# Key maxima of the last tile over all 128 rows with zero-padded keys, bias rows moved from ScalarE's queue to SyncE's, and new order tables

## The chip, the cores and the metric

The kernel runs on one core of a Trainium2 chip. The metric is the device time of one execution in microseconds (us), smaller is better; where several executions are given, their median counts. A core has TensorE (PE, matrix products, with its weight loads shown as PEld), VectorE (DVE), ScalarE (ACT), GpSimd (POOL) and SyncE (SP, which here only issues transfers).

## The reference

A transformer block of two layers over `x` of 2 batches x 1024 tokens x 256 features, fp32.

```python
# layer 0
nx = layer_norm(x, gamma, beta)
weights = softmax((nx @ Wq) @ (ctx @ Wk).T * 256**-0.5)          # over 154 context rows
combined = concat([nx, weights @ (ctx @ Wv), anchor])            # 768 features
probs = softmax(combined @ router_W + router_b)                  # 3 experts
h = silu(combined @ e_w1 + e_b1)                                 # 3 x 512
routed = sum_e((h @ e_w2 + e_b2) * probs)
g = sigmoid(silu(combined @ gate_w1 + gate_b1) @ gate_w2 + gate_b2)
x = x + g * (routed @ out_w + out_b)
# layer 1
xq, xkv = ada_ln(x, cond), ada_ln(ctx, cond)                     # scale and shift from the condition
q, k, v = xq @ Wq + bq, xkv @ Wkv + bkv                          # 16 heads of 16 features
out = softmax(q @ k.T / 4) @ v                                   # per head, 154 keys
return x + (out @ Wp + bp)
```

## The kernel before

The 2048 tokens are worked on in eight tiles of 256, numbered 0 to 7 (`LAST` = 7, `NEXT` = 6; tiles 0 to 3 are batch 0). A product that has to be exact is made as three products of rounded halves into one bank: high by high, high by low, low by high. `exact` issues them, and they are lines L1677, L1678 and L1679 of the trace, whatever the step.

For each tile, TensorE goes through layer 0 (`hidden_banks` and `token_bank`: seven units of 128 x 512 hidden values, which ACT, DVE and POOL turn into `hidden`, `hidden_high`, `hidden_low`), and then through the attention of layer 1, which has these steps:

- `most`: scores of one pair of heads for 128 tokens (308 = 2 x 154 columns) go into a bank of the ring `score_banks` (three banks); DVE reduces them to maxima (`head_maxima`, L1464). There are 16 per tile. For tiles 0 to 6 each is one product over 96 rows (L2020) of stacked queries and keys. For the last tile each is an `exact` of three products over a slice of 32 rows (four pairs of heads share the 128 partitions of `queries_high` and `queries_low`), from `last_keys_high` and `last_keys_low`. This needs no stacked queries.
- `row`: PE transposes the maxima, ACT negates them into a high half and DVE makes the low half. In tiles 0 to 6 SP moves both into four further rows of `query_stack`; in the last tile they stay in `max_halves`.
- `score`: 12 banks of keys x tokens, exponent taken by ACT (L1133) into `exp_ring` (six places). In tiles 0 to 6 a bank takes two products over 100 rows (L2050), the last four rows subtracting the maxima. In the last tile it takes four: two over the 96 rows of `last_query_stack` (L2052) and two over the 40 rows of `max_halves` (L2055), with weights that select a head.
- `value`: products of 32 columns of weights (L2073, L2076) give outputs and sums; ACT copies them out (`raw`). Then comes a chain, mostly on DVE: doubling by a shuffle (L1487), reciprocals of the sums (L1478), spreading and multiplying (L1497, L1499), a rounded copy by ACT (L1149), and its low half by DVE (L1507). Tile 6 does it once, its buffers being named `next_...`; the last tile does it in two halves.
- `proj`, `last`: the output projection and the last addition, then the stores by SP.

In the last tile the queries for `score` are stacked by SP, twelve transfers into `last_query_stack` (L865). `fill` steps (L2119) are products into `token_bank` whose result is never read.

No scheduler orders the work. Each step of each tile has a place, from the tables `PLAN`, `PLAN_OF` (by tile) and `SETUP`, plus an offset per engine from `DELAY`; every engine issues its steps in the order of these numbers. Between engines only semaphores count.

The setup loads weights, builds the context's products, and places four small rows of the first layer's bias (`hidden_bias_high`, `hidden_bias_low`) in `context_w_tail`; ACT issues these four transfers at its start (L929) after waiting for DVE.

Of the kernel before, what the change touches and what calls it, by code (L numbers as in the profile page):

```python
# [12 lines left out]
F32R = mybir.dt.float32r  # L13
# [4 lines left out]
P = 128  # L18
BATCH, SEQ, D, CTX = 2, 1024, 256, 154
KC = D // P  # L20
# [34 lines left out]
MROWS = 32 + HEADS // 2  # L55
# [34 lines left out]
def packed(np, v):  # L90
# [17 lines left out]
    for b in range(BATCH):  # L108
# [133 lines left out]
        "sel": ["s"],  # L242
        "bias": ["x"],
# [7 lines left out]
        "norm": 1.3, "qx": 0.4, "prob": 0.86, "keyx": 0.3, "qx_last": 0.6,  # L251
    },
    "scalar": {
        "cv": -3.8, "ck": -0.1, "fold": 0, "vw": 0.5, "vt": 0.29, "w2": 0.57, "keyx": 0.6, "norm": 1.7, "att": 0.5,
        "logit": 1.61, "z": 0.51, "h": 0.3, "gate": 0.4, "qx": 0.4, "query": -0, "row": 1.16, "score": -0.06,
        "out": 0.3, "xhat_last": -0.1, "qx_last": 0.4, "query_last": 0.2, "row_last": -0.9, "score_last": 0.1,
        "raw_last": -0.2, "out_last": 0.7,
    },
    "vector": {
        "fold": -0.7, "vw": 0.64, "vt": 0.52, "w2": 0.52, "att": 0.1, "route": 0.3, "logit": 1.5, "z": 1.03,  # L260
        "evac": 0.5, "query": 0.1, "most": 0.39, "row": 0.6, "proj": 1.7, "last": -0.3, "key": 0.6, "mod": 0.1,
        "bq": 0.7, "cb": 0.78, "res_last": 0, "qn_last": -1.3, "shift_last": -0.4, "qlow_last": 0.4,
        "query_last": 1.3, "most_last": 1, "row_last": 1.4, "proj_last": -1.1, "dup_last": 0.3, "sums_last": -0.2,
        "out_last": 1.3, "outl_last": -0.5,
    },
    "gpsimd": {
        "h": 0.6, "ln": 0.8, "qn": -0.2, "low": 1, "keyn": 1.4, "split": 1.9,
    },
    "sync": {
        "query": 10.5, "row": -4.5, "proj": -3.6, "last": 0.5, "key": -0.2, "place": 10.8, "query_last": 6.1,  # L270
        "row_last": -1.7, "stack_last": -2.6,
# [9 lines left out]
    "dup": (36.6, 40.5), "za": -0.51, "step": 1.99, "z": 0.3, "h": 1.5, "p": 3.33, "again": -9.3, "vw": -56.6,  # L281
    "ln": -0.16, "norm": 1.7, "low": 11.8, "att": 7.8, "prob": 9.2, "route": 12.1, "logit": 15.01, "res": 17.8,
    "qn": 19, "shift": 19, "xhat": 18.5, "qx": 19.2, "qlow": 19.5, "query": 20.5,
    "most": (21.9, 22.1, 23.6, 25.2, 25.5, 26.9, 27.4, 28.1), "row": (29.46, 39.8), "stack": (13.9, 16.4, 17, 18.6),
    "score": (32, 32.2, 32.5, 32.9, 33.1, 33.9, 34.3, 34.5, 34.5, 34.9, 35.1, 35.6),
    "value": (33.73, 34.8, 35.96, 36.02), "raw": (35.2, 36), "sum": (34.6, 36.5), "sums": (37.4, 44),
    "out": (39.16, 57.16), "outl": (42.3, 93.4), "proj": 44.29, "last": (15.8, 58.6), "reload": 44.8, "init": 6.6,
# [4 lines left out]
        "most": (21.97, 22.93, 23.44, 24.8, 25.52, 26.91, 27.34, 28.59), "res": 17.4, "qn": 17.5, "qx": 18.4,  # L292
        "outl": (43, 97.7),
    },
    1: {
        "row": (28.9, 39.6), "z": 0.6,
    },
    2: {
        "most": (21.91, 22.05, 23.48, 25.2, 25.55, 26.54, 27.45, 28.1),
    },  # L300
    3: {
        "vw": 0.59,
    },
    5: {
        "most": (22.19, 22.37, 23.84, 25.21, 26.15, 27.21, 27.62, 28.43),
    },
    6: {
        "score": (30.81, 30.91, 31.06, 31.5, 31.53, 31.77, 32.08, 32.1, 32.11, 32.67, 32.82, 33.17), "xhat": 17.7,
        "h": 1.3, "qn": 16.8, "z": 0.4, "res": 16.1, "proj": 51.1, "row": (28.9, 36), "raw": (33.1, 35.4),
        "init": 6.2, "p": 3.4, "logit": 13.5, "qx": 18.6, "value": (32, 32.07, 34.38, 34.91), "query": 20.1,  # L310
        "most": (21.9, 22, 24.9, 25.9, 26.7, 27.1, 27.4, 27.7), "step": 1.96,
    },
    7: {
        "most": (19.05, 19.41, 19.52, 19.55, 19.88, 19.93, 20.11, 20.46), "raw": (22.9, 26.5), "xhat": 17.5,
        "proj": 38.1, "sums": (27.1, 32.1), "logit": 14.4, "step": 1.96, "dup": (25.3, 30.1), "h": 1, "prob": 10.6,
        "score": (21.7, 21.8, 21.9, 21.9, 22.2, 22.2, 22.5, 22.9, 23.1, 23.2, 23.2, 23.7), "query": 18.13,
        "qx": 17.31, "row": (20.5, 21.1), "last": (42, 45.3), "value": (22.87, 22.88, 24.09, 24.25), "qlow": 18.9,
        "outl": (35.9, 36), "low": 5.9, "out": (26.2, 31.9), "att": 9, "z": 0.34, "res": 15.6,
# [3 lines left out]
    "vw": (1.3, 3, 3.9, 4, 6.2, 6.4, 8), "vt": (0.7, 2.1, 3.4, 3.7, 4.9, 9.6, 10.6),  # L322
    "unit": (0.3, 2.4, 3.4, 4.3, 7.5, 9.2, 10.1), "w2": (7.3, 10.2, 10.8, 13.2, 14.8, 17.9), "norm": -0.2,
    "low": 2.5, "att": 2.4, "prob": 3.1, "route": 3.9, "logit": 4.4, "cb": 4.05, "bq": 13, "split": (11.1, 15.1),
    "keyn": (8.8, 11.2), "keyx": (12.2, 13.7), "key": (13.9, 17.5), "mod": (9.27, 9.55, 10.38, 10.59), "ck": 11.1,
    "fold": (0.5, 11.9), "late": (9.7, 12.1), "ln": -6.1, "silu": 1.4, "group": 1.9, "gsplit": 3.6, "setup2": -13.2,
    "bias1": -8.1,
    "fill": (120.07, 120.22, 120.24, 120.66, 121.14, 121.3, 122.04, 127.49, 127.92, 128.2, 128.92, 129.37, 129.68, 131.25),
# [1815 lines left out]
```

## Time and profile before

| | before |
|---|---|
| three runs | 467.07, 463.16, 466.98 us |
| median | 466.98 us |
| profiled execution, device time | 464.27 us |
| its span, first to last instruction | 462.1 us |
| mean granted clock of TensorE | 0.956 |

The page's first parts give the busy time of each engine, and the span cut in 40 slices of 11.6 us, each digit a busy share in tenths (for PEclk: the granted clock).

```profile
PE 448.3 (97%) x3629; PEld 396.5 (86%) x3629; DVE 292.1 (63%) x748; ACT 225.7 (49%) x487; POOL 169.7 (37%) x181
PE   7889999999999999999999999999999998899997
PEclk9999999999999999999999999999999999875569
...
query_stack<-queries_high SPq DMA_DIRECT2D x56, 64.0 KB, 2.0
```

The last line is from the list of transfers: their count, KB each, median us from issue to landing.

A busy PE is not the same as a PE at full speed: in the last six slices the busy share stays high, while the clock digits are lower.

### The profile page before, as it was taken

What the parts mean: (1) busy time and instruction counts of PE and PEld (TensorE: products, weight loads), DVE (VectorE), ACT (ScalarE), POOL (GpSimd) and SP (SyncE); (2) the same over time, 40 slices, a digit from 0 to 9 for tenths busy, and PEclk for the clock granted to TensorE, in tenths of its full rate; (3) what the DMA queues carried; (4) which work ended last, traced back from release to release, by engine and by line L of the source; (5) the groups of instructions that cost most, each with busy time, mean ns of one, the idle gap of its engine ahead of it and who ended that gap; (6) DMA issues with size and microseconds to landing.
All of it is one profiled execution on the core that took longest, in us unless ns stands there. A gap on an engine that the chain in (4) does not pass through costs nothing.

```text
span 462.1 us, 9615 instructions
## 1 busy us (share of the span) xinstructions
PE 448.3 (97%) x3629; PEld 396.5 (86%) x3629; DVE 292.1 (63%) x748; ACT 225.7 (49%) x487; POOL 169.7 (37%) x181
## 2 busy tenths in 40 slices
PE   7889999999999999999999999999999998899997
PEld 6578899999998899889989998999899887795556
DVE  1684537754754984589549945975599379355236
ACT  2775644254377446644573466527633743432241
POOL 5355456343441471145414722473432243001000
PEclk9999999999999999999999999999999999875569
DMA  8587212222001301240002001100200022030001
GB/s 311 176 298 261 78 62 59 59 57 53 18 4 23 94 24 35 58 117 1 28 17 76 1 28 38 33 0 27 58 13 4 25 69 57 4 85 7 0 1 45
DMA packets 16517, 27.80 MB, mean 60 GB/s; under 512 B 3736, under 2 KB 8536, under 8 KB 16344
## 3 DMA queue, kind: packets, MB, share of 16 engines
q1 hardware_dynamic: 15832, 27.16, 20.0%
q8 instruction: 29, 0.48, 0.4%
q10 hardware_dynamic: 640, 0.04, 0.1%
q14 instruction: 16, 0.13, 0.1%
HBM read 15.94 MB, written 2.10 MB: 39 GB/s over the span
## 4 chain that ended last, share of the span: by engine, by line
PE 81%; DVE 10%; ACT 4%; issue 2%; DMA 1%; ACTq 1%; SPq 0%
PE hidden_banks L1677 7%; PE hidden_banks L1679 7%; PE hidden_banks L1678 7%; PE token_bank L1677 5%; PE score_banks L2050 5%; PE score_banks L1684 5%; PE token_bank L1678 5%; PE token_bank L1679 5%; PE value_bank L2073 4%; PE score_banks L2020 4%; PE value_bank L2076 3%; PE score_banks L2055 2%; PE score_banks L2052 2%; PE hidden_banks L1902 2%; PE value_bank L1684 2%
## 5 line engine op out<-in xcount | busy, mean ns | idle before, releaser
L1609 POOL TENSOR_TENSOR hidden_low<-hidden,hidden_high 128x512 fp32r<-128x512 f32 x56 | 72.6, 1296 | 134.0 <-ACT hidden_high L1073 133.9
L1133 ACT ACTIVATE exp_ring<-score_banks 128x512 f32<-128x512 f32 x96 | 53.6, 599 | 45.9 <-PE score_banks L2050 28.8
L1464 DVE TENSOR_REDUCE head_maxima<-score_banks 128x2 f32<-128x308 f32 x128 | 54.8, 472 | 17.3 <-PE score_banks L2020 11.4
L1677 PE MATMUL hidden_banks<-normed_high,hidden_w_high 128*128 128x256 f32 x224 | 64.5, 288 | 0.0
L1678 PE MATMUL hidden_banks<-normed_high,hidden_w_low 128*128 128x256 f32 x224 | 62.5, 279 | 0.0
L1679 PE MATMUL hidden_banks<-normed_low,hidden_w_high 128*128 128x256 f32 x224 | 62.4, 279 | 0.0
L1065 ACT ACTIVATE hidden<-hidden_banks 128x512 f32<-128x512 f32 x56 | 33.4, 597 | 50.3 <-PE hidden_banks L1902 50.2
L1677 PE MATMUL token_bank<-expert_out_high,hidden_high 128*128 128x256 f32 x192 | 55.3, 288 | 1.0 <-issue 0.7
L1073 ACT CAST hidden_high<-hidden 128x512 fp32r<-128x512 f32 x56 | 34.7, 620 | 42.2 <-DVE hidden L1381 40.1
L1678 PE MATMUL token_bank<-expert_out_high,hidden_low 128*128 128x256 f32 x192 | 53.5, 279 | 0.0
L1679 PE MATMUL token_bank<-expert_out_low,hidden_high 128*128 128x256 f32 x192 | 53.5, 278 | 0.0
L1381 DVE SCALAR_TENSOR_TENSOR hidden<-hidden,hidden_banks 128x512 f32<-128x512 f32 x56 | 38.2, 682 | 20.6 <-ACT hidden L1065 20.4
L1677 PEld LDWEIGHTS hidden_banks<-normed_high,hidden_w_high 128*128 128x128 f32 x224 | 42.1, 188 | 1.0 <-issue 0.8
L1678 PEld LDWEIGHTS hidden_banks<-normed_high,hidden_w_low 128*128 128x128 f32 x224 | 42.3, 189 | 0.1
L1679 PEld LDWEIGHTS hidden_banks<-normed_low,hidden_w_high 128*128 128x128 f32 x224 | 42.0, 188 | 0.0
L1677 PEld LDWEIGHTS token_bank<-expert_out_high,hidden_high 128*128 128x128 f32 x192 | 36.2, 188 | 1.9 <-issue 1.8
L1678 PEld LDWEIGHTS token_bank<-expert_out_high,hidden_low 128*128 128x128 f32 x192 | 36.2, 189 | 0.1
L1679 PEld LDWEIGHTS token_bank<-expert_out_low,hidden_high 128*128 128x128 f32 x192 | 36.1, 188 | 0.0
L1902 PE MATMUL hidden_banks<-probs_T_tail,context_w_tail 100*128 100x256 f32 x112 | 31.7, 283 | 0.0
L1677 PE MATMUL hidden_banks<-probs_T_high,context_w_high 128*128 128x256 f32 x112 | 31.2, 279 | 0.0
L1679 PE MATMUL hidden_banks<-probs_T_low,context_w_high 128*128 128x256 f32 x112 | 31.2, 279 | 0.0
L1678 PE MATMUL hidden_banks<-probs_T_high,context_w_low 128*128 128x256 f32 x112 | 31.2, 278 | 0.0
(291 smaller groups left out, 1132.8 us busy)
## 6 DMA issues: line engine op xcount, KB each, us to landing
unit_weights<-units SPq DMA_DIRECT2D x7, 768.0 KB, 5.3
query_stack<-queries_high SPq DMA_DIRECT2D x56, 64.0 KB, 2.0
tokens<-x SPq DMA_DIRECT2D x8, 256.0 KB, 4.3
query_stack<-queries_low SPq DMA_DIRECT2D x28, 64.0 KB, 2.0
w_slice<-units SPq DMA_DIRECT2D x7, 256.0 KB, 2.9
out<-tokens SPq DMA_DIRECT2D x7, 256.0 KB, 2.1
w_T<-folds SPq DMA_DIRECT2D x6, 256.0 KB, 5.1
pair_keys<-keys_high SPq DMA_DIRECT2D x16, 77.0 KB
```

The lines of the kernel that those rows point to most:

```text
L1065: nc.scalar.activation(TB[:, ring(t, u), :], Z[:, hidden_bank(t, u), :], ACT.Tanh, scale=0.5).then_inc(scalar_z, 1)
L1073: nc.scalar.copy(SH[:, ring(t, u), :], TB[:, ring(t, u), :]).then_inc(scalar_h, 1)
L1133: nc.scalar.activation(E[:, w % ERING, :], S[:, ring_of[key][0], :], ACT.Exp).then_inc(scalar_score, 1)
L1381: v.scalar_tensor_tensor(out=TB[:, ring(t, u), :], in0=TB[:, ring(t, u), :], scalar=1.0, in1=Z[:, hidden_bank(t, u), :], op0=ALU.add, op1= ...
L1464: v.tensor_reduce(MX[:, s, first:first + step + 1:step], S[:, ring_of[key][0], 0:2 * CTX].rearrange("p (j n) -> p j n", j=2), AX.X, ALU.ma ...
L1609: nc.gpsimd.tensor_tensor(SL[:, ring(t, u), :], TB[:, ring(t, u), :], raw(SH[:, ring(t, u), :]), ALU.subtract).then_inc(gpsimd_h, 1)
L1677: mm(out_, lh, rh, start=start, stop=False, skip_group_check=skip)
L1678: mm(out_, ll, rh, start=False, stop=False, skip_group_check=skip)
L1679: return mm(out_, lh, rl, start=False, stop=stop, skip_group_check=skip)
L1684: last = mm(out_, l, r, start=(i == 0), stop=(i == len(pairs) - 1))
L1902: return mm(half, VWD[0:BROWS, b, c], PTD[0:BROWS, t % 2, :], start=False, stop=True)
L2050: last = mm(bank, left, QS[:, c, :], start=True, stop=True)
```

## The change

Four things change.

1. The maxima of the last tile are products over all 128 rows. The keys of one slice r stand in rows 32r to 32r+31, and zeros in the other rows, so `last_keys_high` and `last_keys_low` are four times as large and lie in other places of the memory. POOL has a new step `zero`, three memsets; SP fills in the keys with twelve transfers in place of eight, after the memsets and no longer after the last hidden unit's products.
2. `MROWS` is `STACK` = 96 and was 40: the products that take the maxima off the last tile's scores (now L2065) go over 96 rows of `max_halves` and of the selecting weights. Rows without a value are zero.
3. SP issues the four bias rows, between the loads of the second and third unit of weights, and waits for DVE there; ACT does not.
4. All tables have new numbers. The number of computing steps is the same; their order differs in many places.

```diff
-MROWS = 32 + HEADS // 2
+MROWS = STACK
 STEPS["gpsimd"]:
+        "zero": ["h", "l0", "l1"],
 DELAY, PLAN, PLAN_OF, SETUP: new numbers throughout, for instance
-        "most": (19.05, 19.41, 19.52, 19.55, 19.88, 19.93, 20.11, 20.46), "raw": (22.9, 26.5), "xhat": 17.5,
+        "route": 13.2, "most": (19.2, 19.2, 19.3, 19.4, 19.4, 19.6, 20.3, 20.5), "init": 5.6, "sums": (28.4, 36),
...
-    "sel": 115.5, "unstack": 112.2, "bias2": (33.8, 37),
+    "sel": 114.7, "unstack": 105, "bias2": (26.4, 26.7), "zero": 102.7,
...
-        LKH, LKL, after = run(weights_at + 2 * 4 * KC * ZCOLS, [
-            ("last_keys_high", [P, KC, 2, CTX], F32R), ("last_keys_low", [P, KC, 2, CTX], F32R)])
+        LKH = put("last_keys_high", [P, KC, GROUPS, 2 * CTX], F32R, offset=keys_at)
+        LKL = [put("last_keys_low0", [P, GROUPS, 2 * CTX], F32R, offset=slices_at),
+               put("last_keys_low1", [P, GROUPS, 2 * CTX], F32R, offset=xhat_at)]
...
-            return NMS[0:PAIRS, h, :], NMS[32:MROWS, h, :], PAIRS
+            return NMS[0:PAIRS, h, :], NMS[32:32 + PAIRS, h, :], PAIRS
... SP, the loads at the start
                 unit_load(1)
+                sp.wait_ge(vector_bias1, upto(vector_bias1, ("bias1", 0), "b"))
+                for i, part in enumerate((BRH, BRL)):
+                    for b in range(BATCH):
+                        row = STACK + 2 + i
+                        sp.dma_start(raw(VWD[row:row + 1, b, :]), raw(part[:, :])).then_inc(bias_placed, 16)
                 unit_load(2)
... SP
             def unstack(key):
-                sp.wait_ge(tensor_z, upto(tensor_z, ("z", LAST, NU - 1), "z"))
-                for dst, first in ((LKH, 0), (LKL, 64)):
-                    for r in range(GROUPS):
-                        sp.dma_start(raw(dst[32 * r:32 * r + 32, :, :, :]),
-                                     raw(KS[1][first:first + 32, 2 * r:2 * r + 2, :, :])).then_inc(last_keys_placed, 16)
+                sp.wait_ge(gpsimd_zero, upto(gpsimd_zero, key, "l1"))
+                for r in range(GROUPS):
+                    rows = slice(32 * r, 32 * r + 32)
+                    sp.dma_start(raw(LKH[rows, :, r, :]), raw(KS[1][0:32, 2 * r:2 * r + 2, :, :].rearrange("p f j n -> p f (j n)"))).then_inc(
+                        last_keys_placed, 16)
+                    for f in range(KC):
+                        sp.dma_start(raw(LKL[f][rows, r, :]),
+                                     raw(KS[1][64:STACK, 2 * r + f, :, :].rearrange("p j n -> p (j n)"))).then_inc(last_keys_placed, 16)
... ACT: the step bias_rows, with the same wait and the same four transfers, is gone
... POOL
+            def zeros(key):
+                p = nc.gpsimd
+                pool.wait_ge(tensor_score, upto(tensor_score, ("score", TPB - 1, SCORES - 1), "s"))
+                p.memset(raw(LKH[:, :, :, :]), 0.0).then_inc(gpsimd_zero, 1)
+                pool.wait_ge(tensor_vw, upto(tensor_vw, ("vw", 1, NU - 1), "m"))
+                p.memset(raw(LKL[0][:, :, :]), 0.0).then_inc(gpsimd_zero, 1)
+                pool.wait_ge(tensor_prob, upto(tensor_prob, ("prob", LAST), "p"))
+                pool.wait_ge(tensor_att, upto(tensor_att, ("att", LAST), "s"))
+                pool.wait_ge(gpsimd_low, upto(gpsimd_low, ("low", LAST), "n"))
+                p.memset(raw(LKL[1][:, :, :]), 0.0).then_inc(gpsimd_zero, 1)
... PE, the maxima of the last tile
-                        pe.wait_ge(last_keys_placed, 16 * 2 * GROUPS)
+                        pe.wait_ge(last_keys_placed, 16 * (1 + KC) * GROUPS)
...
                     r, f = divmod(c, 2)
-                    rows, columns = slice(32 * r, 32 * r + 32), slice(P * s, P * s + P)
-                    keys_high, keys_low = (k[rows, f, :, :].rearrange("p j n -> p (j n)") for k in (LKH, LKL))
-                    exact(bank, (QH[rows, f, columns], QL[rows, f, columns]), (keys_high, keys_low), True, True).then_inc(tensor_most, 1)
+                    columns = slice(P * s, P * s + P)
+                    exact(bank, (QH[:, f, columns], QL[:, f, columns]), (LKH[:, f, r, :], LKL[f][:, r, :]), True, True).then_inc(tensor_most, 1)
```


What the tables do is seen in the order of the instructions. First PE, end of the last tile's scores (`score_banks`) and values (`value_bank`), before, and then with the change:

```order
L2052 MATMUL score_banks<-last_query_stack,pair_keys_67 128x256
L2055 MATMUL score_banks<-max_halves,head_rows_of_tails 128x256
L2073 MATMUL value_bank<-exp_ring,head_values_69 32x256 x4
L2076 MATMUL value_bank<-exp_ring,head_values_tail_71 32x256 x4
L2073 MATMUL value_bank<-exp_ring,head_values_69 32x256 x4
L2076 MATMUL value_bank<-exp_ring,head_values_tail_71 32x256 x4
L2119 MATMUL token_bank<-proj_w_high 128x256 x28
L2084 MATMUL head_bank<-proj_w_high,next_outs_low 128x256
L2085 MATMUL head_bank<-proj_w_low,next_outs_low 128x256
```

```order
L2065 MATMUL score_banks<-max_halves,head_rows_of_tails 128x256
L2129 MATMUL token_bank<-proj_w_high 128x256 x4
L2083 MATMUL value_bank<-exp_ring,head_values_69 32x256 x4
L2086 MATMUL value_bank<-exp_ring,head_values_tail_71 32x256 x4
L2083 MATMUL value_bank<-exp_ring,head_values_69 32x256 x4
L2086 MATMUL value_bank<-exp_ring,head_values_tail_71 32x256 x4
L2129 MATMUL token_bank<-proj_w_high 128x256 x20
L2094 MATMUL head_bank<-proj_w_high,next_outs_low 128x256
L2095 MATMUL head_bank<-proj_w_low,next_outs_low 128x256
L2097 MATMUL head_bank<-second_bias,bias_rows 128x256
```

Four of the filling products now stand ahead of the second half's values, and 20 rather than 28 behind them; the values themselves are unchanged. The order of the three kinds of work is the same.

POOL in the last tile's layer 0 (`probs` is the router's, `hidden_low` that of the hidden units), before and with the change:

```order
L1632 TENSOR_TENSOR probs<-exps,softmax_small 128x2x128
L1633 TENSOR_TENSOR probs<-exps,softmax_small 128x2x3x26
L1609 TENSOR_TENSOR hidden_low<-hidden,hidden_high 128x512 x3
L1535 TENSOR_TENSOR rstd_84<-mean_var_83,minus_half 128x2
```

```order
L1643 TENSOR_TENSOR probs<-exps,softmax_small 128x2x128
L1644 TENSOR_TENSOR probs<-exps,softmax_small 128x2x3x26
L1620 TENSOR_TENSOR hidden_low<-hidden,hidden_high 128x512 x2
L1588 MEMSET last_keys_high 128x2464
L1590 MEMSET last_keys_low_153 128x1232
L1594 MEMSET last_keys_low_154 128x1232
L1620 TENSOR_TENSOR hidden_low<-hidden,hidden_high 128x512 x3
L1534 TENSOR_TENSOR rstd_84<-mean_var_83,minus_half 128x2
```

The three memsets stand between the low halves of the second and the third of these units.

SP in the loads at the start, before and with the change:

```order
L804 DMA query_score_w_raw<-query_score_w 128x512
L794 DMA unit_weights<-units 128x1536 x3
L808 DMA out_w_raw<-out_w 128x512
L809 DMA gate_out_raw<-gate_out 128x512
L810 DMA second_bias_full<-gate_rows 32x256
```

```order
L803 DMA query_score_w_raw<-query_score_w 128x512
L793 DMA unit_weights<-units 128x1536 x2
L811 DMA context_w_tail<-hidden_bias_high 1x112x16 x2
L811 DMA context_w_tail<-hidden_bias_low 1x112x16 x2
L793 DMA unit_weights<-units 128x1536
L813 DMA out_w_raw<-out_w 128x512
L814 DMA gate_out_raw<-gate_out 128x512
```

The four bias rows now stand ahead of the third of the unit loads, and `out_w` and everything behind it come after them.

## Rows read from the trace of the kernel before

**Rows 1.** Windows of TensorE: stretch, length, busy (instructions), granted clock, DMA share, GB/s.

```profile
60.00:393.00 333.00, 329.68 (x2835) 1.00 0.15 37
396.70:399.90 3.20, 3.20 (x17) 0.52 0.00 0
407.00:410.00 3.00, 3.00 (x21) 1.00 0.27 62
410.00:415.00 5.00, 5.00 (x27) 0.50 0.56 143
424.00:436.00 12.00, 12.00 (x24) 0.50 0.00 0
```

**Rows 2.** Timeline, PE, tile 6 scores, last tile's first maxima products: start, length, engine, line, operation.

```profile
395.72 1.16 PE L2050 MATMUL score_banks<-query_stack,pair_keys 100*128 100x256 f32 x6 [1.65 <-DMA query_stack<-max_low]
...
407.35 0.37 PE L1677 MATMUL score_banks<-last_keys_high,queries_high 32*128 32x308 f32 x1
...
408.13 0.30 PE L1679 MATMUL score_banks<-last_keys_low,queries_high 32*128 32x308 f32 x1
```

**Rows 3.** Timeline, DVE, reductions of the last tile's maxima [idle before].

```profile
411.99 0.48 DVE L1464 TENSOR_REDUCE head_maxima<-score_banks 128x2 f32<-128x308 f32 x1 [0.29 <-PE score_banks L1679]
412.76 1.42 DVE L1464 TENSOR_REDUCE head_maxima<-score_banks 128x2 f32<-128x308 f32 x3 [0.29 <-PE score_banks L1679]
```

**Rows 4.** Timeline, PEld (weight loads), start of the last tile's scores.

```profile
422.33 0.33 PEld L2052 LDWEIGHTS score_banks<-last_query_stack,pair_keys 96*128 96x128 f32 x1
422.89 0.28 PEld L2055 LDWEIGHTS score_banks<-max_halves,head_rows 40*128 40x128 f32 x1 [0.22 <-issue]
423.40 0.29 PEld L2052 LDWEIGHTS score_banks<-last_query_stack,pair_keys 96*128 96x128 f32 x1 [0.23 <-issue]
```

**Rows 5.** Timeline, PE, maxima of tile 6, and the last filling products.

```profile
388.18 0.59 PE L2020 MATMUL score_banks<-pair_keys,query_stack 96*128 96x308 f32 x3
...
451.43 3.61 PE L2119 MATMUL token_bank<-proj_w_high 128*128 128x256 f32 x28
```

**Rows 6.** Timeline, ACT, exponentials of tile 6.

```profile
403.67 1.58 ACT L1133 ACTIVATE exp_ring<-score_banks 128x512 f32<-128x512 f32 x3 [1.40 <-PE score_banks L2050]
```

**Rows 7.** Chain that ended last, 400 to 449 us: start, length, what.

```profile
402.28 0.43 PE value_bank L2073 x8
...
438.59 0.85 PE value_bank L2073 x8
...
443.31 0.31 PE score_banks L2055
```

**Rows 8.** Timeline, DVE, the chains of tile 6 and of the last tile's halves.

```profile
423.69 1.30 DVE L1487 STREAM_SHUFFLE next_outs_twice<-outs_and_sums 128x1024 f32<-128x1024 f32 x1
...
428.57 1.23 DVE L1499 TENSOR_TENSOR next_outs_twice<-next_outs_twice,next_sums_spread 128x1024 f32<-128x1024 f32 x1
440.99 0.73 DVE L1487 STREAM_SHUFFLE last_outs_twice<-last_outs_and_sums 128x512 f32<-128x512 f32 x1
...
444.40 0.69 DVE L1499 TENSOR_TENSOR last_outs_twice<-last_outs_twice,last_sums_spread 128x512 f32<-128x512 f32 x1
449.98 1.28 DVE L1507 SCALAR_TENSOR_TENSOR next_outs_low<-next_outs_high,constants,next_outs_twice 128x1024 fp32r<-128x1024 f32 x1 [4.89 <-ACT next_outs_high L1149]
452.21 0.74 DVE L1487 STREAM_SHUFFLE last_outs_twice<-last_outs_and_sums 128x512 f32<-128x512 f32 x1
```

**Rows 9.** Timeline, SP, the last of 12 copies of the last tile's queries.

```profile
414.82 0.59 SPq L865 DMA_DIRECT2D last_query_stack<-queries_high  x1
```

**Rows 10.** Timeline, POOL: a memset of 512 columns, and a low half.

```profile
2.13 0.53 POOL L1543 MEMSET head_values_tail<- 128x512 f32 x1
...
347.52 1.30 POOL L1609 TENSOR_TENSOR hidden_low<-hidden,hidden_high 128x512 fp32r<-128x512 f32 x1 [3.36 <-ACT hidden_high L1073]
```

**Rows 11.** Timeline, the setup: PE's third context product, ACT's first copy.

```profile
8.17 1.21 PE L1684 MATMUL hidden_banks<-context_and_key_w,context_and_value_w 128*128 128x154 f32 x8
...
9.49 0.37 ACT L940 COPY values_T<-score_banks 128x256 f32<-128x256 f32 x1
```

More of the change, by code:

```diff
@@ L261 @@
[L261 to L264, printed above, removed]
+        "fold": -0.6, "vw": 0.6, "vt": 0.6, "w2": 0.6, "att": 0.2, "route": 0.4, "logit": 1.6, "z": 1, "evac": 0.5,
+        "query": 0, "most": 0.43, "row": 0.4, "proj": 2.5, "last": -0.2, "key": 0.6, "mod": 0.1, "bq": -0.3, "cb": 0,
@@ L265 @@
+        "res_last": -1.5, "qn_last": -1.3, "shift_last": -1.1, "qlow_last": 1, "query_last": 1.1, "most_last": 1.5,
+        "row_last": 1.2, "proj_last": -10.8, "dup_last": 0.7, "sums_last": -1.6, "out_last": 1.4, "outl_last": 1.4,
     },
     "gpsimd": {
-        "h": 0.6, "ln": 0.8, "qn": -0.2, "low": 1, "keyn": 1.4, "split": 1.9,
+        "h": 0.6, "ln": 0.86, "qn": -0.2, "low": 0.9, "keyn": 1.2, "split": 2.1,
     },
     "sync": {
-        "query": 10.5, "row": -4.5, "proj": -3.6, "last": 0.5, "key": -0.2, "place": 10.8, "query_last": 6.1,
@@ L271 @@
-        "row_last": -1.7, "stack_last": -2.6,
+        "query": 13.4, "row": -3.6, "proj": 1.5, "last": -2.1, "key": -0.9, "place": 11.3, "query_last": 3.7,
+        "row_last": -3.6, "stack_last": 1.9,
     },
@@ L280 @@
 PLAN = {
[L281 to L287, printed above, removed]
+    "dup": (37.2, 49.2), "za": -0.4, "step": 1.99, "z": 0.38, "h": 1.5, "p": 3.3, "again": -6.4, "vw": -38.8,
+    "ln": 0.2, "norm": 1.6, "low": 6.6, "att": 7.9, "prob": 9.1, "route": 12.3, "logit": 14.4, "res": 17.4,
+    "qn": 18.4, "shift": 18.5, "xhat": 19.3, "qx": 19.54, "qlow": 20.1, "query": 20.7,
+    "most": (22.11, 22.29, 23.89, 24.92, 26.01, 26.34, 27.35, 28.05), "row": (29.2, 30.6),
+    "stack": (15.3, 16.8, 20.9, 23.1),
+    "score": (32, 32.1, 32.1, 32.7, 33.5, 33.7, 34.2, 34.3, 34.3, 35.4, 35.5, 35.6),
+    "value": (33.88, 34.18, 35.92, 36.25), "raw": (35.5, 36.9), "sum": (35.3, 36.4), "sums": (38.1, 47.7),
+    "out": (38.34, 56.69), "outl": (43.37, 97.85), "proj": 43.6, "last": (16, 59.3), "reload": 45.3, "init": 5.2,
 }
@@ L291 @@
     0: {
[L292 to L299 removed]
+        "most": (21.92, 23.13, 24.17, 24.59, 25.33, 27.11, 27.44, 28.14), "qlow": 19.3, "query": 19.9, "qn": 17.5,
+        "h": 1.3, "qx": 18.7, "xhat": 18.2,
+    },
+    1: {
+        "logit": 15.4, "z": 0.62,
@@ L300 @@
     },
     3: {
[L302 removed]
+        "vw": 0.9,
     },
     5: {
[L305 removed]
+        "value": (33.8, 34.8, 35.8, 36),
     },
     6: {
[L308 to L310 removed]
@@ L311 @@
-        "most": (21.9, 22, 24.9, 25.9, 26.7, 27.1, 27.4, 27.7), "step": 1.96,
-    },
-    7: {
-        "most": (19.05, 19.41, 19.52, 19.55, 19.88, 19.93, 20.11, 20.46), "raw": (22.9, 26.5), "xhat": 17.5,
[L315 to L318, printed above, removed]
+        "init": 6.5, "score": (30.5, 30.6, 30.6, 31.3, 31.4, 31.6, 31.9, 31.9, 31.9, 32.5, 32.6, 33),
@@ new lines @@
+        "raw": (34.4, 34.5), "proj": 47.7, "most": (21.9, 22, 24.8, 25.8, 26.5, 27.3, 27.4, 28), "ln": 0.9,
+        "value": (31.83, 31.84, 34.15, 34.75), "norm": 1.79, "stack": (16.3, 16.7, 21.5, 21.9),
+    },
+    7: {
+        "route": 13.2, "most": (19.2, 19.2, 19.3, 19.4, 19.4, 19.6, 20.3, 20.5), "init": 5.6, "sums": (28.4, 36),
+        "za": -0.73, "score": (22.06, 22.59, 22.73, 23.07, 23.16, 23.16, 23.63, 23.73, 24.03, 24.23, 24.34, 24.54),
+        "outl": (33.4, 33.8), "row": (19.96, 21.53), "h": 1.2, "p": 3.5, "last": (39.5, 39.7), "query": 18.06,
+        "xhat": 17.7, "ln": 0.5, "value": (23.2, 23.5, 24.7, 25.8), "proj": 38, "logit": 14.9, "out": (27.3, 33.2),
+        "raw": (23.1, 28.7), "qlow": 18, "qx": 17.62, "dup": (24.9, 28.7), "step": 1.96,
```

41 lines of the change are left out of this document (17 added, 24 removed).

## The prediction

> **What bounds the kernel now.** I read the shares first: PE is busy 97% of the span, DVE 63%, the others less, so anything that doesn't shorten PE's work, or the chain that hangs on it at the end, is worth little. The window from 60 to 393 us confirms it for the eight layer-0 stages: 329.7 of 333 us busy at full clock [rows 1]. All reordering in there can win at most the 3.3 us of idle time.
>
> The clock line and the windows show another thing. The granted clock is full (2.4 GHz) up to 393 us, and half (1.2 GHz) in three places of the last 70: from 396.7 to 399.9, after PE had stood still for 1.65 us, and then from 410 on, while PE never stood still: 5.00 of 5.00 and 12.00 of 12.00 us busy at 0.50 [rows 1, 2]. The second fall begins about 3 us into the last tile's maxima. Those are products over 32 rows; just before it they run at full clock, six from 407.35 to 408.13, 0.16 us apart [rows 2]. With the half clock DVE gets a bank every 0.77 us (411.99 to 412.76), though it can reduce one in 0.47 (three in 1.42) [rows 3].
>
> Then the last tile's scores. Two weight loads start 422.33 and 423.40 with one product between, 0.54 us for each load and product, and each load waits ("issue") until the product before is over [rows 4]. Products of one shape don't do that: three over 96 rows take 0.59 us, 28 over 128 rows take 3.61 (0.13 each) at full clock [rows 5]. So before, these 48 products pay for load and product, one after the other, and at half clock. ACT is no bound there: it could take a bank every 0.5 us (three in 1.58) [rows 6]. The values double with the clock too: eight in 0.43 us at 402.28, in 0.85 at 438.59 [rows 7].
>
> What comes after is DVE's: tile 6's chain from 423.69 to 429.80 (6.1 us), that of half 0 from 440.99 to 445.09 (4.1), a low half of 1.28, and half 1, whose first shuffle starts at 452.21, 9.9 us ahead of the end [rows 8]. This last piece has PE nearly idle.
>
> **Edit 1, maxima over 128 rows.** The number of products (48) and of columns (308) stays, so at equal clock they cost the same: a product over 96 rows is as long as one over 32 (0.59 for three against 0.78 for six with starts 0.16 apart) [rows 2, 5]. What can change is the clock. All that ran at full clock for 333 us had 96 to 128 rows; what was running when it fell without idle time had 32 [rows 1]. I take it that full rows hold the clock. Then DVE is the bound: first bank 0.7 us after 407.35 (two distances of 0.16 and the length of one product), 16 reductions at 0.47 are 7.6, and the last ends near 415.6. The transposes for half 1 end near 416, so scores start at 416.3 and not 422.33: 6 us. Against the same edit at half clock, 0.
>
> **Edit 2, 96 rows for both kinds of score products.** All four products of a bank now have one shape. By the pitch in [rows 5] the loads are then hidden: 0.12 to 0.2 us per product and not 0.54, and a bank's four are 0.5 to 0.8. At full clock a bank takes 4 x 0.12, and ACT's 0.5 decides: twelve banks in about 6 us, 32 values 4 x 0.43 = 1.7, and about 1.5 for the places where a value product waits for the exponential just before it. Values end near 425.8, ACT's copy near 426.5; before, 451.4.
>
> The saving of 25 us in PE isn't had in full, since **DVE becomes the bound**. The second row of maxima is ready near 416.9. From there DVE has tile 6's chain (6.1, to 423.0), half 0 (4.1, to 427.1), the low half (1.3, to 428.4), and then half 1, whose copy is there since 426.5. From its first shuffle it is the same 9.9 us: 438.3, against 462.1. That is -23.8. ACT's cast for the low half falls at 423 to 424.3, after its exponentials and beside half 0's chain. PE's fills in front of the values (8 x 0.13 = 1 us) lie in that slack.
>
> The last of the twelve query copies is issued by SP at 414.82 + 0.59 [rows 9]; the page's row on these transfers, quoted with the shares, gives 2.0 us to landing, so 417.4. Scores start at 416.3 with group 0, and the last group is needed some 4 us later: hidden, by 3 us.
>
> **POOL's zeros.** 128 x 512 in 0.53 us [rows 10] gives 9.6 x 0.53 = 5.1 us for 4928 columns. They stand between two low halves; POOL waits 3.36 us there for ACT [rows 10]. 5.1 - 3.4 = 1.7 us late for one low half, whose product comes a unit later. I take 0 and keep 1.7 as the other end. The twelve key transfers (12 x 0.6 = 7.2 us of SP) are issued some 30 us before the maxima need them.
>
> **Edit 3, bias rows.** Ahead of ACT's first copy, at 9.49 [rows 11], stand five issues of transfers and a table load. Four of them are now gone, 2.4 us by the 0.6 that an issue takes on SP [rows 9], up to 3 with their wait; but the third context product ends only at 9.38 [rows 11], and SP now waits for DVE ahead of the third unit's weights. Bounds -3 to +1; I take -1, nearest to the row that limits it. The other moves within the setup go with it.
>
> **Tables.** In the middle 0, within -2 (of 3.3 idle) and +2.
>
> **Sum.** -23.8 - 1 + 0 + 0 = -24.8 against the profiled execution of 464.27 (span 462.1): 439.5. The median of the three runs is 466.98, and of the four times two are near 464 and two near 467. I take half the difference, 1.4: **441 us**.
>
> **Rivals.**
>
> *B, one half of the gain.* Either the clock falls again when the scores begin (96 rows may be too few: 396.7 to 399.9 had 100-row products and 128-row fills at 0.52, though after an idle stretch [rows 1, 2]), or it holds, but loads of the alternating sources still are not hidden. In the first case a bank takes 4 x 0.22 = 0.88 (the part of the 0.54 that is not the load and its start [rows 4]), 12 are 10.6, values 3.4, fills and waits 3: first shuffle of half 1 at about 433.4, span 443.3, time 445.5. In the second, 48 x 0.31 (the start distances in the short warm stretch near 443.31 [rows 7]) is 14.9 and half 1 starts at 435: 447. Against it is that before, all 96- and 128-row stretches were at full clock. Chance 0.18.
>
> *C, the clock falls all the same, in the maxima.* What falls at 410 may be something other than the rows, the short waits for DVE's banks perhaps. Then only edit 2 gains: reductions at 0.77, scores from 420.9, 10.6 + 3.4 + 3.5, half 1 at 439.5, span 449.4 and with the setup 450.4 to 452. Chance 0.12. The Trainium skill ("TensorE: Matmul & The Clock Gate", Loop structure matters more than you think) ties a warm clock to back-to-back products and to no gaps in PE's work. By that rule, padding rows would bring nothing, as the stretches at 0.50 already are 100% busy, and the time would be that of C; the trace agrees with it at 396.7, and disagrees at 410.
>
> *D, slower.* If the loads of products over the same rows aren't hidden, the maxima pay what the scores pay today, 0.54 each, once the slices of 32 rows are gone: 48 x 0.54 = 25.9 against the 12.3 that they take now, +13.6 us: 478. It decides from a pitch above 0.3. In the same page, Part 3 (What overlaps and what doesn't), the Trainium skill says that a weight load runs beside a product only when their row groups differ, and by it the forecast of edit 2 would fall as well. The rows speak against it: 96-row products take 0.59 for three, and 128-row fills 0.13 each, all on the same partitions [rows 5]. Chance 0.03.
>
> *E, no change.* The new order loses elsewhere what the end wins, by a wait of PE for a late low half in each of seven units, or a stop after the zeros: 24 us would be needed. Chance 0.03. The remaining 0.64 are the forecast's.
>
> **How the numbers follow.** The forecast's own range is 436 to 444: setup -3 to +1, middle +-2, zeros up to 1.7, and 1.4 for the choice of the base. The range 435 to 452 takes in B and C, and leaves out D, E and some of the forecast's edge. About 1% (4.7 us) is what a measurement can tell from no change here. Faster by more than that: the forecast, B and C, 0.94; within 1%: 0.03; slower: 0.03.
>
> **What the profile after would show.** The clock line at 9 to the end; the last tile's reductions without gaps, 0.47 apart, with PE at 1.00; score products 0.12 apart and weight loads without "issue" before them; DVE without idle time from tile 6's shuffle to half 1's, with half 1's at about 428 and the end 9.9 later; ACT's first copy near 9; no low half of POOL later than ACT's cast by over 2 us. I'm wrong if the clock is at 0.5 anywhere after 407, or if DVE waits between the chains, for then the 6.1 + 4.1 + 1.3 isn't the bound but the values.

## The result

The changed kernel takes 438.88 us (median of four runs, 438.0 to 439.08), against 467.02 for the kernel before (four runs). The ratio is 0.941, 95% interval 0.936 to 0.946: faster, by 28 us in the medians. The prediction said 441 us, 435 to 452. The profiled execution took 439.08 with a span of 436.9, against the predicted 439.5 on the profiled execution; the span is 25.2 us shorter. The medians differ by more than the spans because the profiled execution of the kernel before (464.27) was one of its faster ones, and that of the changed kernel the slowest of its four.

The page of the changed kernel, its first two parts (shares, the busy digits of PE, the clock digits; a slice is now 10.9 us):

```profile
PE 422.1 (97%) x3629; PEld 384.7 (88%) x3629; DVE 296.3 (68%) x748; ACT 223.6 (51%) x487; POOL 175.0 (40%) x184
PE   7899999999999999999999999999999899979996
PEclk9999999999999999999999999999999999998999
```

PE's busy time fell by 26 us though it does the same number of products, and the clock digits are 9 but for one. The windows of PE, for the stretches that answer to [rows 1]: length, busy (instructions), granted clock, DMA share, GB/s.

```profile
60.00:393.00 333.00, 327.07 (x2818) 1.00 0.16 41
391.00:393.60 2.60, 1.01 (x9) 1.00 0.06 11
394.00:398.00 4.00, 4.00 (x24) 0.58 0.20 68
398.10:437.00 38.90, 35.13 (x338) 1.00 0.13 35
```

From 398.1 to the end the clock is full; before, the stretch from 400 on held over 35 us at half clock. The one fall left is that of [rows 1] at 396.7, two microseconds earlier. It follows the same wait of 1.67 us for the transfer of tile 6's maxima.

The last tile's maxima on PE and their reductions on DVE, timeline of the changed kernel, against [rows 2, 3]:

```profile
405.38 0.31 PE L1688 MATMUL score_banks<-last_keys_high,queries_high 128*128 128x308 f32 x1
...
406.09 0.30 PE L1690 MATMUL score_banks<-last_keys_low,queries_high 128*128 128x308 f32 x1
```

```profile
406.01 5.30 DVE L1463 TENSOR_REDUCE head_maxima<-score_banks 128x2 f32<-128x308 f32 x12 [0.82 <-PE score_banks L1690]
411.45 0.41 DVE L1470 SCALAR_TENSOR_TENSOR max_halves<-score_banks,max_halves 8x256 fp32r<-8x256 f32 x1
412.68 1.74 DVE L1463 TENSOR_REDUCE head_maxima<-score_banks 128x2 f32<-128x308 f32 x4 [0.81 <-PE score_banks L1690]
```

A product over 128 rows is 0.14 us from the next, as one over 32 was while the clock was full: the padding itself costs nothing. Twelve reductions stand without a gap in 5.30 us, 0.44 each; there is one gap of 0.81 where PE put values between.

The scores on PE: first the first score product of the kernel before, then the changed kernel, against [rows 4]:

```profile
422.40 0.56 PE L2052 MATMUL score_banks<-last_query_stack,pair_keys 96*128 96x256 f32 x1
```

```profile
414.97 0.36 PE L2062 MATMUL score_banks<-last_query_stack,pair_keys 96*128 96x256 f32 x1
415.17 0.28 PE L2065 MATMUL score_banks<-max_halves,head_rows 96*128 96x256 f32 x1
415.29 0.28 PE L2062 MATMUL score_banks<-last_query_stack,pair_keys 96*128 96x256 f32 x1
...
425.66 0.61 PE L2086 MATMUL value_bank<-exp_ring,head_values_tail 128*32 128x256 f32 x8
426.20 2.66 PE L2129 MATMUL token_bank<-proj_w_high 128*128 128x256 f32 x20
```

The distance from one product to the next is 0.12 us. Scores and values run from 414.97 to 426.2, where the fills begin: 11.2 us, and 29.0 before (422.40 to 451.43 [rows 5]). DVE from the second row of maxima to the shuffle of half 1, against [rows 8]:

```profile
415.85 0.41 DVE L1470 SCALAR_TENSOR_TENSOR max_halves<-score_banks,max_halves 8x256 fp32r<-8x256 f32 x1 [1.44 <-ACT max_halves L1121]
...
416.31 1.33 DVE L1486 STREAM_SHUFFLE next_outs_twice<-outs_and_sums 128x1024 f32<-128x1024 f32 x1
...
422.00 0.75 DVE L1486 STREAM_SHUFFLE last_outs_twice<-last_outs_and_sums 128x512 f32<-128x512 f32 x1
...
425.95 1.28 DVE L1506 SCALAR_TENSOR_TENSOR next_outs_low<-next_outs_high,constants,next_outs_twice 128x1024 fp32r<-128x1024 f32 x1
427.15 0.75 DVE L1486 STREAM_SHUFFLE last_outs_twice<-last_outs_and_sums 128x512 f32<-128x512 f32 x1
```

None of these rows has an idle bracket after the first: DVE works without a gap for 10.9 us, and the end comes 9.8 us behind the last shuffle. ACT's copy of half 1, which that shuffle needs as well, is over only 0.2 us ahead of it (426.93 and 427.15):

```profile
426.34 0.59 ACT L1142 COPY last_outs_and_sums<-value_bank 128x512 f32<-128x512 f32 x1 [0.74 <-PE value_bank L2086]
```

So DVE is the bound, but PE's values and this copy follow right behind it.

So the 25.2 us of span come from: 2.0 up to the first maximum (405.38 and 407.35), 5.5 from there to the first score product (9.6 and 15.1 us), 17.6 from there to half 1's shuffle (12.2 and 29.8), 0.1 behind it.

### The profile page after: what moved, and what is told of

It reads as the page before. It is cut to its first block, busy times and chain, and to the rows that moved or that the text cites. A ratio compares the mean times of both kernels' runs of the same rounds, so it can differ in the third digit from the quotient of the medians.

```text
span 436.9 us, 9623 instructions
## 1 busy us (share of the span) xinstructions
PE 422.1 (97%) x3629; PEld 384.7 (88%) x3629; DVE 296.3 (68%) x748; ACT 223.6 (51%) x487; POOL 175.0 (40%) x184
## 4 chain that ended last, share of the span: by engine, by line
PE 77%; DVE 15%; issue 3%; ACT 3%; DMA 1%; SPq 1%; ACTq 0%
PE hidden_banks L1688 7%; PE hidden_banks L1690 7%; PE hidden_banks L1689 7%; PE score_banks L1695 6%; PE score_banks L2060 5%; PE token_bank L1688 5%; PE token_bank L1689 5%; PE token_bank L1690 5%; PE score_banks L2030 4%; PE value_bank L2083 3%; PE value_bank L2086 3%; PE value_bank L1695 3%; DVE head_maxima L1463 3%; PE hidden_banks L1913 2%; DVE sums L1477 2%
## 5 line engine op out<-in xcount | busy, mean ns | idle before, releaser
L1132 ACT ACTIVATE exp_ring<-score_banks 128x512 f32<-128x512 f32 x96 | 52.6, 600 | 18.8 <-PE score_banks L2060 17.5
L2030 PE MATMUL score_banks<-pair_keys,query_stack 96*128 96x308 f32 x112 | 29.4, 335 | 2.5 <-DVE head_maxima L1463 1.4
```

Source lines behind the costliest of these rows:

```text
L1132: nc.scalar.activation(E[:, w % ERING, :], S[:, ring_of[key][0], :], ACT.Exp).then_inc(scalar_score, 1)
L2030: mm(bank, QS[0:STACK, c, P * s:P * s + P], KS[b][0:STACK, c, :, :].rearrange("p j n -> p (j n)"), start=True, stop=True).then_inc(tensor_ ...
```

## The experiments

The theory: two things held the end back. Products over 32 rows let the clock fall (edit 1), and the 96-row and 40-row products, taken in turns, could not hide each other's weight loads, which costs time by itself and lets the clock fall too (edit 2). The first rival: the new tables brought the gain. The second: the clock does not depend on how many rows a product has. Ratios are against the kernel before, run beside each group of experiments on the same chip: 465.39 us beside the runs with 40, 32 and 64 rows and edit 2 alone, 465.65 beside both undone, the bias rows, the first run with more fills and the scores with 64 rows, 466.21 beside the rest. The changed kernel itself (438.88) was measured beside 467.02. The kernel before thus moved by up to 1.6 us between the groups, and differences of medians from the changed kernel are good to about that.

### Edit 2 undone

```
-MROWS = STACK
+MROWS = 32 + HEADS // 2
```

> The changed kernel, with only the maxima's products of the last tile's scores back at 40 rows. My theory: loads of products whose row counts differ (96, 40) are not hidden. Maxima stay at full clock (reductions 0.47 apart); a score product then takes 0.31 us if the clock holds (48 x 0.31 = 14.9, scores and values end about 6 us later, 445 us), or 0.51 if it falls (48 x 0.51, about 18 us later, 457). I expect the fall, 455 to 458. Rival, the gain is from the tables: 439, with half 1's first shuffle at 427.

Measured 455.29 us, ratio 0.981 (0.975 to 0.988). PE, timeline and windows of this run:

```profile
413.39 0.36 PE L2062 MATMUL score_banks<-last_query_stack,pair_keys 96*128 96x256 f32 x1
413.69 0.38 PE L2065 MATMUL score_banks<-max_halves,head_rows 40*128 40x256 f32 x1
414.00 0.38 PE L2062 MATMUL score_banks<-last_query_stack,pair_keys 96*128 96x256 f32 x1
```

```profile
404.00:412.00 8.00, 8.00 (x65) 1.00 0.42 95
414.00:419.00 5.00, 5.00 (x18) 1.00 0.00 0
420.00:426.00 6.00, 6.00 (x38) 0.50 0.00 0
```

The distance is 0.31 us at full clock and not 0.12, and after some 6 us of it the clock falls, with nothing but these products before it. It came back once, at 426.1 behind four groups of value products, and fell again at 429.5 among products of 96 and 40 rows. Edit 2 is worth 16.4 us with edit 1 in place.

### Edit 1 undone, and the maxima over 64 rows

In the first, the maxima read the rows of their slice alone, in the second the slice and its neighbour's zeros:

```
+rows = slice(32 * r, 32 * r + 32)                      # e2_slices32
+rows = slice(64 * (r // 2), 64 * (r // 2) + 64)        # e3_rows64
-exact(bank, (QH[:, f, columns], QL[:, f, columns]), (LKH[:, f, r, :], LKL[f][:, r, :]), True, True)
+exact(bank, (QH[rows, f, columns], QL[rows, f, columns]), (LKH[rows, f, r, :], LKL[f][rows, r, :]), True, True)
```

> The changed kernel, but the last tile's maxima are products over 32 rows again, from the same padded keys (the zero rows are not read). My theory: the clock falls about 3 us into the maxima, a reduction every 0.77 us instead of 0.47, +4.8 us; if the 96-row scores bring it back the time is 444, if they don't, a bank of scores takes 0.88 instead of 0.5 and it is 450. Rival (the clock does not depend on rows): clock as in the changed kernel, 439.

> The changed kernel with the maxima over 64 rows (two slices, one of them zeros). Same number of products and columns as with 32 and 128. If the granted clock follows the rows in use gradually or by a bound between 32 and 64, this is as fast as the changed kernel, 439; if the bound is above 64 rows, it equals the run with 32 rows, 444 to 450. I expect 439. Rival (clock does not depend on rows): 439 too, then the run with 32 rows is 439 as well.

Measured 443.31 us with 32 rows (ratio 0.953, 0.948 to 0.958) and 437.92 with 64 (0.942, 0.937 to 0.946). The windows from 405 to 409 and from 410 to 419 us of PE, first with 32 rows, then with 64:

```profile
405.00:409.00 4.00, 4.00 (x30) 1.00 0.44 101
410.00:419.00 9.00, 9.00 (x54) 0.50 0.12 27
```

```profile
405.00:409.00 4.00, 4.00 (x30) 1.00 0.48 109
410.00:419.00 9.00, 8.83 (x99) 1.00 0.13 30
```

This tells the theories of the clock apart. Up to 409 both runs issue the same products in the same order, 0.14 us apart and without a gap, at full clock. Then the run with 32 rows falls to half and the one with 64 does not. The one gap of the latter, 0.17 us, comes only at 414.9, in its scores. Rows decide here and not gaps. The second thing seen is that 64 rows would have done: no measured difference between 64 and 128. With 32 rows the fall came at 409.8, when twelve of sixteen banks were done and value products ran, later than I had put it, and the clock was back at 1.00 by 420, in the 96-row scores that began at 416.5; that is why undoing edit 1 alone costs only 4.4 us.

### Edit 2 alone in the kernel before

```
-MROWS = 32 + HEADS // 2
+MROWS = STACK
-return NMS[0:PAIRS, h, :], NMS[32:MROWS, h, :], PAIRS
+return NMS[0:PAIRS, h, :], NMS[32:32 + PAIRS, h, :], PAIRS
```

> The kernel before, with only the maxima's products of the last tile's scores over 96 rows instead of 40. My theory: loads are hidden; the maxima keep the half clock of before (scores start at 422.3), then 48 products of 0.22 (10.6 us) and 32 values (3.4) and about 2 of waits at half clock instead of 29.1 us: 454 us; if 96-row products bring the clock back, 450. Rival (the order tables are the gain): 467.

Measured 446.02 us, ratio 0.959 (0.954 to 0.965): 19.4 us for one constant, more than I expected. PE's windows show why:

```profile
410.00:423.00 13.00, 13.00 (x73) 0.50 0.18 42
424.00:432.00 8.00, 8.00 (x97) 1.00 0.01 2
```

The clock is at half in the maxima, as before, and comes back at about 423.2, in the scores that began at 420.4 (0.21 us from product to product at half clock, 0.12 after). I had left open whether it would, with 450 for yes. Of the other 4 us, 2.0 are that the traced execution had no fall at 396.7 and started its scores at 420.4 and not 422.4; the rest was not taken apart.

### Both undone

The edits of the first two experiments (40 rows, and 32 rows for the maxima) together.

> The changed kernel with edits 1 and 2 both undone: maxima over 32 rows, maxima's products of the scores over 40. What is left is the new tables, the bias rows on SP and the (now unused) zeroing. My theory: both undone cost at least the sum of each alone (16.4 and 4.4), 438.9 + 20.8 = 460, and up to 465 because the clock that stays low from the maxima meets the unhidden loads. Rival, the tables hold a large share of the gain: below 455.

Measured 462.99 us, ratio 0.993 (0.991 to 0.996): the tables and the bias rows on SP are worth 2.7 us of the 27. The two edits together are worth 24.1 and each alone 16.4 and 4.4, which leaves 3.3 for both at once, not much more than the 1.6 us that these differences are good to. Seen from this run, edit 1 alone brings 7.7 (to 455.29) and edit 2 alone 19.7 (to 443.31). The rival that the tables made the gain is refuted.

### Why the loads were not hidden: 64 and 72 rows

```
+MROWS = 64        # e9_mrows64
+MROWS = 72        # e10_mrows72
```

> The changed kernel with the maxima's products of the last tile's scores over 64 rows, against 96 of the stack products between them. If a weight load is hidden only between products that use the same part of the rows, or that both are over 64, the pitch is 0.31 as with 40 rows and the time about 455. If all that matters is that 40 isn't a multiple of 32, it is 0.12 and 439. I expect 0.31, 455.

> The changed kernel with the maxima's products of the last tile's scores over 72 rows, between stack products over 96: different counts, neither a multiple of the other nor of 32, but both over 64. If loads are hidden wherever both products have over 64 rows (as those over 100 and over 128 do beside each other), the pitch is 0.12 and the time 439. If row counts must be equal, 0.31 and 455 to 457, as with 40 and 64 rows. I expect 439.

Measured 457.09 us with 64 rows (ratio 0.982, 0.978 to 0.987) and 438.96 with 72 (0.942, 0.937 to 0.947). Weight loads with 64 rows, then with 72:

```profile
415.72 0.19 PEld L2062 LDWEIGHTS score_banks<-last_query_stack,pair_keys 96*128 96x128 f32 x1
416.04 0.18 PEld L2065 LDWEIGHTS score_banks<-max_halves,head_rows 64*128 64x128 f32 x1
416.35 0.19 PEld L2062 LDWEIGHTS score_banks<-last_query_stack,pair_keys 96*128 96x128 f32 x1
```

```profile
415.01 0.19 PEld L2062 LDWEIGHTS score_banks<-last_query_stack,pair_keys 96*128 96x128 f32 x1
415.12 0.19 PEld L2065 LDWEIGHTS score_banks<-max_halves,head_rows 72*128 72x128 f32 x1
415.24 0.19 PEld L2062 LDWEIGHTS score_banks<-last_query_stack,pair_keys 96*128 96x128 f32 x1
```

A load takes 0.19 us in both. With 72 rows the next begins 0.12 later, while the one before still runs; with 64 rows it begins 0.31 later, the 0.19 of the load and the 0.12 of a product one after the other. Row counts need not be equal (96 and 72), nor be multiples of 32 (72), and a multiple of 32 doesn't help (64). What fits all four settings is that both products lie above 64 rows. Two 64-row products beside each other do hide their loads, as the maxima over 64 rows show:

```profile
404.35 0.30 PE L1690 MATMUL score_banks<-last_keys_low,queries_high 64*128 64x308 f32 x1
404.49 0.29 PE L1688 MATMUL score_banks<-last_keys_high,queries_high 64*128 64x308 f32 x1
```

So it is the change from one kind to the other that costs.

### The bias rows on ACT again

```
-sp.dma_start(raw(VWD[row:row + 1, b, :]), raw(part[:, :])).then_inc(bias_placed, 16)     # between unit_load(1) and (2)
+act.dma_start(raw(VWD[row:row + 1, b, :]), raw(part[:, :])).then_inc(bias_placed, 16)    # ACT, after its first transfer
```

> The changed kernel with the four bias rows issued by ACT again, at its start after the table load's place, all else the same. The setup won 2.7 us between the two profiles (first layer-0 units). If ACT's issues are the cause, ACT's first copy goes from 6.5 back to about 9.5 and the time to 441.5. If the setup's tables are the cause, 439 (+0 to +0.5).

Measured 439.59 us, ratio 0.945 (0.942 to 0.949); the intervals of this and the changed kernel overlap. ACT's first copy in the changed kernel, then in this run:

```profile
6.48 0.37 ACT L939 COPY values_T<-score_banks 128x256 f32<-128x256 f32 x1 [3.62 <-PE score_banks L1695]
```

```profile
8.87 0.37 ACT L942 COPY values_T<-score_banks 128x256 f32<-128x256 f32 x1
```

The first copy is 2.4 us later with the rows on ACT, yet the first layer-0 unit only 0.3 (29.68 and 30.01). Most of that was slack. By elimination, and from one trace each, the setup's 2.9 us came mainly from the setup's tables.

### More fills in PE's wait

```
-FILLS = 14
+FILLS = 17
-"fill": (120.23, 120.27, ...
+"fill": (119.1, 119.12, 119.14, 120.23, 120.27, ...
```

> The changed kernel with three more filling steps (12 products, about 1.4 us) in the 1.67 us in which PE waits for the transfer of tile 6's maxima. My theory: PE's idle time there is what lets the clock fall for 3 us in some executions (two of six profiled traces show it); with the fills it falls in none, and every execution is at the lower of the two times seen, about 438.0 instead of 438.0 to 439.1. Rival: the stretch is bound by ACT's exponentials and the query chain, no difference in the median, 438.9; a loss would show as the fills ending after the transfer has landed, +0.2.

> The run with three more filling steps again, as the base of the two that follow on this chip: 437.7, clock 1.00.

Measured 437.69 us (six runs, ratio 0.940, 0.938 to 0.943), with a mean clock of 1.00 in all six; on the repeat 438.44 (0.941, 0.937 to 0.945), with 1.00 in three of six and 0.992 in three. PE in the first of them:

```profile
391.72 1.60 PE L2129 MATMUL token_bank<-proj_w_high 128*128 128x256 f32 x12
393.56 0.98 PE L2060 MATMUL score_banks<-query_stack,pair_keys 100*128 100x256 f32 x6 [0.24 <-DMA query_stack<-max_low]
```

The wait is 0.24 in place of 1.67 and the scores start when they did. But that no execution would see a fall is refuted; where it fell in those three was not seen, they have no trace. Beside that repeat the kernel nearest to the changed one (72 rows) took 438.96, so a gain of half a microsecond is likely and not shown.

### What sets the end: more work for DVE, less for PE

Both start from the kernel with 17 fills. In one, tile 6's low half is worked out once more into a dead buffer; in the other two fills among the second half's scores are gone.

```
+if t == NEXT:                                           # e11_outl_twice
+    v.scalar_tensor_tensor(out=LKL[0][:, :, 0:TILE], in0=raw(high[:, g, :]), scalar=..., in1=twice[:, g, :], ...)
-FILLS = 17; "fill": (..., 121.98, 127.05, 127.63, 128.86, ...)
+FILLS = 15; "fill": (..., 121.98, 128.86, ...)          # e12_fewer_fills
```

> The kernel of e8_fills_in_wait, in which DVE works out tile 6's low half twice at the end (once into a dead buffer), 1.28 us more on DVE ahead of half 1's first shuffle. If DVE's chain from the last row of maxima is what sets the end, all of it shows: 437.7 + 1.2 = 438.9, half 1's shuffle 1.2 us later. Rival, that PE's scores and values or ACT's copy set it, with slack on DVE: +0.

> The kernel of e8_fills_in_wait without the two filling steps (8 products, 1 us) among and behind the second half's scores. If DVE sets the end, values come up to 0.8 us earlier and the time stays 437.7 (-0.1 to +0.1), provided that the clock stays at 1.00. If PE set the end, 436.7 to 437.0. If those fills hold the clock, it falls near the end: 438.5 or more.

Measured 440.44 us with more DVE work (ratio 0.946, 0.942 to 0.950), 437.93 with fewer fills (0.940, 0.936 to 0.944), against 438.44 for their base beside them. DVE's rows, base, more work, fewer fills:

```profile
426.02 0.76 DVE L1486 STREAM_SHUFFLE last_outs_twice<-last_outs_and_sums 128x512 f32<-128x512 f32 x1
```

```profile
424.83 1.28 DVE L1507 SCALAR_TENSOR_TENSOR last_keys_low<-next_outs_high,constants,next_outs_twice 128x1024 fp32r<-128x1024 f32 x1
426.02 1.76 DVE L1509 SCALAR_TENSOR_TENSOR next_outs_low<-next_outs_high,constants,next_outs_twice 128x1024 fp32r<-128x1024 f32 x1
427.72 0.73 DVE L1486 STREAM_SHUFFLE last_outs_twice<-last_outs_and_sums 128x512 f32<-128x512 f32 x1
```

```profile
426.24 0.74 DVE L1486 STREAM_SHUFFLE last_outs_twice<-last_outs_and_sums 128x512 f32<-128x512 f32 x1
```

DVE's extra work moved the last shuffle by 1.70 us and the time by 2.0, so there is no slack on DVE. The second of the two operations took 1.76 us instead of 1.28; why, stays open. The rest of it fits the clock: PE waits 2.11 us for DVE near the end, its base 0.90, and then gets 0.69 where its base gets 1.00. PE's windows, more DVE work and then the base:

```profile
431.00:438.00 7.00, 3.17 (x18) 0.69 0.22 75
```

```profile
431.00:435.80 4.80, 2.17 (x18) 1.00 0.33 109
```

Less work on PE brought ACT's copy for half 1 forward by 0.6 us (425.21 to 424.61) and the shuffle not at all. DVE is the bound from the second row of maxima on, as the sum took it; in the base ACT's copy is over 0.2 us ahead of the shuffle (425.80 and 426.02), so PE has no more slack than that.

## Why the prediction was right

**Edit 1** was put at 6 us up to the scores' start; it is 5.5 there. Its reason held: rows, not gaps. The reductions were even a little faster (0.44 in place of 0.47). The predicted stretch had no room for the value products that PE puts between the 12th and the 13th reduction, with a gap of 0.81.

**Edit 2** had no price of its own, since the sum followed the path: scores from 0.54 to 0.12 us apart, measured 0.12; values ending at 425.8, measured 426.2; and then DVE as the bound. That the values ended where they were put is luck. The first maximum came 2.0 us earlier than the sum assumed, and scores and values took 11.2 us and not 9.5. The sum had 1.7 us for the values ("4 x 0.43"), but there are two halves of four such groups: they took 1.9 each (418.49 to 420.35 and 424.34 to 426.20). So the slack that it gave PE against DVE, 1.9 us (copy 426.5, shuffle 428.4), was 0.2. The DVE chain was put at 11.5 us (416.9 to 428.4) and took 10.9; the second row of maxima came 10.9 us behind the first product of the maxima, put at 9.6. These two leave the end short by 0.7. The two edits were predicted as one path and the experiments now split them: edit 2 16.4 to 19.7 us, edit 1 4.4 to 7.7.

**Rivals.** B and C needed a fall of the clock after 407: there is none. But both mechanisms are real. The unhidden loads of B are what 40 and 64 rows show, and the clock's return in the 96-row scores, which B doubted, is what makes edit 2 so strong alone. C priced "only edit 2 gains" at 450.4 to 452; the run that is exactly this (edit 1 undone) took 443.3, because C kept half clock through the scores. C was the rule of the Trainium skill ("TensorE: Matmul & The Clock Gate", Loop structure matters more than you think). A window 9.00 of 9.00 us busy at 0.50, beside 8.83 of 9.00 busy at 1.00, goes against it here: gaps were not the cause of that fall. The fall behind the wait of 1.65 us agrees with it. D, loads not hidden over the same rows, is refuted by 128-row products 0.14 apart. The rule of the Trainium skill behind it ("TensorE: Matmul & The Clock Gate", Part 3, What overlaps and what doesn't) lets a weight load overlap only when row groups differ. It does not tell the four settings apart: all of them share rows with the 96-row products, and beside 96 and 72 the loads are hidden, beside 40 and 64 not.

**Setup** was put at -1 and is -2.9 at the first layer-0 unit (32.59 and 29.68). The step that failed: I let ACT's first copy wait for the third context product, ending at 9.38. It waits for the first one, and starts at 6.48. And the reason was wrong as well: of the gain only 0.3 us at that unit belongs to the bias rows, the rest to the setup's tables, which the sum had lumped in.

**Middle** was put at 0 and is +0.9: the first maximum comes 2.0 us earlier and not 2.9. PE waits more in the maxima of tiles 0 to 6, 1.4 us in six pieces for DVE (0.5 before) and 0.9 for a transfer of stacked queries. It also stands still for 0.8 us at 343.25, ahead of the last tile's first unit, until DVE's last step of the router's part is over at 343.16. That these waits are the cause is argued from the two traces and was not tried. The errors partly cancel, and that is luck: -1.9 from the setup, +0.9 from the middle and +0.6 at the end (-23.2 and not -23.8) leave 0.4.

**The base.** The sum gives 439.5, and 1.4 were added for the median. The changed kernel's four times lie within 1.1 us, and its traced one was the slowest of them, so this term was not needed: of the 2.1 us between 441 and 438.88 it is the larger part.

**POOL's zeros** took 4.4 us, estimated 5.1; the next low half follows at once, some 2 us after its input (342.40 + 0.62 and 344.90). None of PE's waits around them ends with POOL: between 338 and 358 they are 0.20 and 0.29 for DVE's maxima and the 0.79 at 343.25. The units' first ACT step leads the kernel before by 2.2 us ahead of the zeros (331.58 and 333.78) and by 2.2 behind them (353.63 and 355.83), so 0 was right as far as these two traces tell.

## What to carry to other kernels

Look at TensorE's clock by window before shortening its work: a fully busy stretch at 0.50 was here one of products over 32 rows, or of products whose weight loads were not hidden, and rows of zeros, which cost nothing per product, kept the clock up in both. Keep products that take turns in one class of row counts, all above 64 or none: in these runs each change of class showed the weight load in full (0.31 us against 0.12). And once such a stretch shrinks, follow the next engine's chain from its start: here it ended 0.2 us behind PE's, and taking 8 more products off PE did not move the last shuffle.

## What the runs showed of the hardware

- The granted clock fell to 0.50 in stretches with no idle time and few rows: maxima over 32 rows, 0.14 us apart; with 64 rows it stayed at 1.00. It fell as well in products over 96 and 40 rows, 0.31 apart, though the engine counts as busy there too; why, the runs do not show.
- It came back while scores over 96 rows with hidden loads ran without a pause: at 423.2 after a start at 420.4 (edit 2 alone), and by 420 after 416.5 (edit 1 undone). It also came back for 3.4 us behind groups of value products, at 441.0 in the kernel before and at 426.1 with edit 2 undone, and both times fell again in products 0.31 apart.
- The same wait of 1.6 to 1.7 us was followed by a stretch of 3.4 us at half clock in four of the ten traces that have it (before, changed, and scores with 64 and with 72 rows) and by none in the other six (40 rows, 32 and 64 rows for the maxima, edit 2 alone, both undone, bias rows on ACT). So one trace can't tell whether such a wait costs the clock; it makes about 1 us of the spread between executions (the changed kernel took 438.0 at a mean clock of 1.00, and 438.7 to 439.1 at 0.992 to 0.996). Two traces also have such a stretch in the setup: edit 2 alone from 27.4 us on (3.4 us), both undone from 11.9 on (6.8 us).
- 96-row products beside 72-row ones: 0.12 us each; beside 64-row ones: 0.31.
